# One attention and expert kernel: third softmax's exponentials as stationary f16 halves, values ahead of the last query tiles, constant products in TensorE's waits

## The reference

```python
x = x + layernorm(attention(layernorm(x), w_qkv, w_proj))
x = x + layernorm(ffn(layernorm(x), ...))       # base product + one of 8 adapters, by smallest loss

# attention, per batch and head
Q, K, V = split(x @ w_qkv);  Q = Q / 4
Q_l, K_l = means of 16 successive tokens of Q, K          # 64 landmarks
kernel1 = softmax(Q   @ K_l.T)      # 1024 x 64
kernel2 = softmax(Q_l @ K_l.T)      # 64 x 64
kernel3 = softmax(Q_l @ K.T)        # 64 x 1024, the third softmax
SV  = (kernel1 @ iterative_inv(kernel2)) @ (kernel3 @ V)  # 6 Newton steps
out = SV @ w_proj
```

## Time and profile before

| | |
|---|---|
| median of three runs | 2275.7 us (2271.61 to 2277.06) |
| the profiled execution | 2281.05 us, of which its span 2279.3 us |
| TensorE matmul busy | 2019.9 us, 89% of the span |
| DVE / ACT / POOL busy | 1471.1 (65%) / 864.9 (38%) / 700.9 us (31%) |
| mean granted TensorE clock | 0.964 of full speed |
| chain that ended last | TensorE 62%, DVE 17%, SP's queue 9%, issue 4%, ACT 3%, POOL 3%, DMA 2% |
| period of a batch | 134.5 us, from the reciprocal L1549, which starts at 94.5 us in the first batch and at 2112.2 us in the last, 15 periods later |

### The profile page before, as it was taken

One profiled execution on the slowest core, in us unless ns is written; L12 is line 12 of the kernel. 1 busy time (PEld: TensorE's weight loads), 2 busy tenths in 40 slices (PEclk: granted clock), 3 DMA queues, 4 the chain that ended last, 5 costly groups with the idle time before them and its releaser, 6 DMA issues.

```text
span 2279.3 us, 58742 instructions
## 1 busy us (share of the span) xinstructions
PE 2019.9 (89%) x24991; PEld 1307.2 (57%) x24991; DVE 1471.1 (65%) x3319; ACT 864.9 (38%) x1509; POOL 700.9 (31%) x916
## 2 busy tenths in 40 slices
PE   3888989999898998989899898989989898998945
PEld 1554747556474755647465564746657475665724
DVE  3667576766757667675766757576675757767531
ACT  3334344343433443343343434334343443334320
POOL 4153152322315232232523224251331424223051
PEclk9889999999999999999999999999999999999978
DMA  6213141221514222151422215132231513213020
GB/s 152 46 47 76 30 122 39 81 61 30 121 30 116 44 73 61 29 131 30 112 44 71 66 30 131 30 99 52 63 79 30 129 31 89 62 41 83 11 56 19
DMA packets 232972, 150.71 MB, mean 66 GB/s; under 512 B 153035, under 2 KB 203732, under 8 KB 232693
## 3 DMA queue, kind: packets, MB, share of 16 engines
q1 hardware_dynamic: 232710, 146.95, 27.5%
HBM read 36.98 MB, written 16.78 MB: 24 GB/s over the span
## 4 chain that ended last, share of the span: by engine, by line
PE 62%; DVE 17%; SPq 9%; issue 4%; ACT 3%; POOL 3%; DMA 2%; DVEq 1%; POOLq 0%; ACTq 0%
PE NS L979 11%; PE ringF L1187 9%; SPq L429 9%; PE ringF L1172 6%; PE KV L1060 5%; PE ringA L1146 5%; PE ringA L880 5%; PE ringF L1220 3%; PE ringA L1046 3%; PE ringA L1022 3%; DVE stage L1608 3%; DVE mx L1518 2%; PE ringF L880 2%; PE ringF L1222 2%; ACT E L690 2%
## 5 line engine op out<-in xcount | busy, mean ns | idle before, releaser
L1187 PE MATMUL ringF<-x,H 128*128 128x256 f16 x1536 | 237.9, 273 | 0.0
L1532 DVE TENSOR_REDUCE mx<-ringA 128x8 f32<-128x512 f32 x256 | 175.4, 685 | 89.3 <-PE ringA L1022 88.8
L682 ACT ACTIVATE E<-ringA,score_scale 128x512 f32<-128x512 f32 x256 | 175.5, 686 | 116.8 <-PE ringA L1046 116.7
L1187 PE MATMUL ringF<-H 128*128 128x128 f16 x1024 | 204.4, 220 | 1.4 <-DVE H L1619 1.4
L880 PE MATMUL ringA<-xT,wqkv 128*128 128x512 f16 x768 | 184.0, 391 | 21.2 <-ACT QS L700 11.7
L1585 DVE SCALAR_TENSOR_TENSOR X<-X,NS 128x320 f32<-128x320 f32 x160 | 78.0, 488 | 182.8 <-PE NS L979 177.7
L1518 DVE TENSOR_REDUCE mx<-ringA 128x1 f32<-128x512 f32 x256 | 160.1, 682 | 52.0 <-PE ringA L1013 51.5
L1172 PE MATMUL ringF<-wd,x2T 128*128 128x512 f16 x768 | 187.9, 384 | 6.4 <-DVE H L1619 3.1
L516 POOL TENSOR_SCALAR vtmp<-mv,eps_ffn 128x8 f32<-128x8 f32 x16 | 5.1, 316 | 612.0 <-DVE mv L1363 612.0
L690 ACT ACTIVATE E<-ringA,score_scale 128x512 f32<-128x512 f32 x256 | 158.6, 684 | 75.2 <-PE ringA L1077 75.2
L516 POOL TENSOR_SCALAR vtmp<-mv,eps_ln 128x8 f32<-128x8 f32 x32 | 9.9, 310 | 538.2 <-DVE mv L1363 538.2
(11 more groups left out here) (261 smaller groups left out, 4317.8 us busy)
## 6 DMA issues: line engine op xcount, KB each, us to landing
KS<-stage SPq DMA_DIRECT2D x384, 64.0 KB, 2.0
QS<-stage SPq DMA_DIRECT2D x384, 64.0 KB, 2.0
xin<-in_L_attn_x_dram SPq DMA_DIRECT2D x16, 1024.0 KB, 11.0
xres<-in_L_attn_x_dram SPq DMA_DIRECT2D x16, 1024.0 KB, 8.1
...
```

The costliest lines, as they stand in the source:

```text
L682: A(E[:, k % ESLOTS, :], ps[:, :], ACT.Exp, scale=score_scale[:, 0:1]).then_inc(freed["s3"].sem, 1)
L1187: ins = MM(dst, H[:, a, t, own], src, start=first and i == 0, stop=last and i >= 3, skip_group_check=True)
L1532: V_.reduce_max(mx1[:, t, 8 * h:8 * h + 8], take(b, "m1", k)[:, :].rearrange("p (a m) -> p a m", a=8), AX.X)\
```

## The change

It does seven things.

- The third softmax's exponentials come twice from ACT: once as f16 (`E16`, four slots that lie in `yout`) and once as f32 (`E`), from the same bank. POOL subtracts the first from the second and writes the low half (`exponentials_lo`).
- POOL splits the values into two f16 halves with a column of ones behind (`values16`, `V16`). The f32 `V` now lies in slots 4 to 7 of `E`.
- `sum_values` has the halves of `E` as stationary operands (128 x 128, f16) and the values as moving ones: per step 4 products of 65 columns and 4 of 33, into `KV` for the first eight steps and `NS[1]` for the last. It waits for POOL's low half and stands three steps behind the scores instead of two, and the first `gram` goes before its last two steps.
- The end: DVE copies the sums out (`values_take`, 128 x 260, twice, the first in step 11), adds two parts, and multiplies by the reciprocal of 8 columns. The big reciprocal, its product, TensorE's two transposes and the copies are gone. The small products of the denominators move from `NS[1]` to free columns of `KV`.
- `pv` 2 and 3 go after `m3` 3 and 7, `pk` 6 and 7 after `m3` 7 and 9. ACT's order follows: both values before `halves2` of the first group.
- Constant products that nobody reads (`keep_warm`, identity times 512 weight columns; `stir`, 128 columns) are put ahead of most `m3`, at the scores' steps 1, 2 and 4, in steps 11 to 14, and at the start and end of the kernel.
- ACT's `halves1` go from Newton steps 0 and 1 to 1 and 2.

```diff
@@ -114,6 +116,7 @@
...
+        E16 = yout[:, :, :].bitcast(F16).rearrange("p t c -> p (t c)").rearrange("p (s h n) -> p s h n", s=4, h=2)
...
@@ -123,8 +126,9 @@
...
-        V = sb("V", [P, T, PAIRS, HD2])
+        V16 = sb("V16", [P, T, PAIRS, 2 * HD2 + 2], F16)
         E = sb("E", [P, ESLOTS, HALF])
+        V = E[:, 4:8, :].rearrange("p k n -> p (k n)").rearrange("p (t a d) -> p t a d", t=T, a=PAIRS)
...
@@ -172,9 +179,8 @@
...
-                  + [("m3", k) for k in range(4)] + [("pk", 6), ("m3", 4), ("pk", 7)]
-                  + [("m3", k) for k in range(5, 9)] + [("pv", 2)] + [("m3", k) for k in range(9, 13)] + [("pv", 3)]
-                  + [("m3", k) for k in range(13, 16)] + [("f3", 0)])
+                  + [("m3", k) for k in range(4)] + [("pv", 2)] + [("m3", k) for k in range(4, 8)] + [("pv", 3), ("pk", 6)]
+                  + [("m3", 8), ("m3", 9), ("pk", 7)] + [("m3", k) for k in range(10, 16)] + [("f3", 0)])
...
@@ -561,6 +569,29 @@
...
+            def values16(b):
+                for k in range(4):
+                    rows = slice(2 * k, 2 * k + 2)
+                    pool.wait_ge(freed["pv"].sem, freed["pv"].at(b, k + 1))
+                    pool.sem_inc(s_apart, 1)
+                    if k == 0 and not first(b):
+                        pool.wait_ge(kv_full.sem, kv_full.at(b - 1, 2 * T))
+                        pool.sem_inc(s_apart, 1)
+                    pool.tensor_copy(V16[:, rows, :, HD2:2 * HD2], V[:, rows, :, :]).then_inc(v16.sem, 1)
+                for g in range(2):
+                    rows = slice(4 * g, 4 * g + 4)
+                    pool.wait_ge(v16.sem, v16.at(b, 4 + g))
+                    pool.sem_inc(s_apart, 1)
+                    pool.tensor_tensor(V16[:, rows, :, 0:HD2], V[:, rows, :, :], V16[:, rows, :, HD2:2 * HD2],
+                                       ALU.subtract).then_inc(v16.sem, 1)
+
+            def exponentials_lo(b):
+                for k in range(16):
+                    pool.wait_ge(freed["s3"].sem, freed["s3"].at(b, k + 1))
+                    pool.sem_inc(s_apart, 1)
+                    pool.tensor_tensor(E16[:, k % 4, 1, :], E[:, k % ESLOTS, :], E16[:, k % 4, 0, :], ALU.subtract)\
+                        .then_inc(e_lo.sem, 1)
...
             def body(b, more):
                 if not first(b):
                     norm2(b - 1)
+                values16(b)
+                exponentials_lo(b)
                 if more:
                     norm1(b + 1)
...
@@ -678,13 +711,20 @@
             def exp3(b, k):
                 ps = take(b, "s3", k)
                 if k >= ESLOTS:
-                    act.wait_ge(kv_full.sem, kv_full.at(b, k - ESLOTS + 1))
+                    act.wait_ge(e_lo.sem, e_lo.at(b, k - ESLOTS + 1))
+                elif k == 4:
+                    act.wait_ge(v16.sem, v16.at(b, 6))
+                if k >= 4:
+                    act.wait_ge(kv_full.sem, kv_full.at(b, k - 4 + 1))
+                elif k == 0 and not first(b):
+                    act.wait_ge(x2lo.sem, x2lo.at(b - 1, 2))
+                A(E16[:, k % 4, 0, :], ps[:, :], ACT.Exp, scale=score_scale[:, 0:1])
                 A(E[:, k % ESLOTS, :], ps[:, :], ACT.Exp, scale=score_scale[:, 0:1]).then_inc(freed["s3"].sem, 1)
...
@@ -752,12 +792,12 @@
                 values(b, (0, 1))
                 landmark_stack(b)
                 staged(b, (2,))
+                values(b, (2, 3))
                 if ffn:
                     halves2(b - 1, (0,))
                 staged(b, (3,))
                 if ffn:
                     halves2(b - 1, (1,))
-                values(b, (2, 3))
...
@@ -787,8 +827,8 @@
                     if k == 3:
                         exp1(b, 6)
                         exp1(b, 7)
-                    if more and k < 2:
-                        halves1(b + 1, (k,))
+                    if more and 1 <= k < 3:
+                        halves1(b + 1, (k - 1,))
...
@@ -890,6 +930,16 @@
...
+            def keep_warm(cols, times=1):
+
+                for _ in range(times):
+                    MM(NS[1][:, 0:cols], ident[:, :], wqkv[:, 0, 0, 0:cols], start=True, stop=True)
+
+            def stir(times):
+
+                for _ in range(times):
+                    MM(NS[1][:, 264:392], ident[:, :], wqkv[:, 0, 0, 0:P], start=False, stop=False, skip_group_check=True)
...
             def project(b):
+                if first(b):
+                    keep_warm(512, 10)
...
@@ -1049,24 +1101,20 @@
             def sum_values(b, k):
 
                 g, t = k // T, k % T
-                pe.wait_ge(freed["s3"].sem, freed["s3"].at(b, k + 1))
+                pe.wait_ge(e_lo.sem, e_lo.at(b, k + 1))
                 if k == 0:
-                    pe.wait_ge(freed["pv"].sem, freed["pv"].at(b, 4))
+                    pe.wait_ge(v16.sem, v16.at(b, 6))
                     if not first(b):
-                        pe.wait_ge(w_done.sem, w_done.at(b - 1, 3))
-                for i in range(2):
-                    for j in range(GP):
-                        p = g * GP + j
-                        ins = MM(KV[32 * j:32 * j + 32, (2 * g + i) * P:(2 * g + i + 1) * P], onesf[:, :] if i else V[:, t, p, :],
-                                 E[:, k % ESLOTS, j * P:(j + 1) * P], start=t == 0 and i == 0, stop=t == T - 1,
-                                 skip_group_check=True)
+                        pe.wait_ge(w_done.sem, w_done.at(b - 1, 4))
+                acc_bank = (KV, NS[1])[g]
+                for j in range(GP):
+                    p = g * GP + j
+                    cols = slice(j * P, (j + 1) * P)
+                    MM(acc_bank[:, j * VW:(j + 1) * VW], E16[:, k % 4, 0, cols], V16[:, t, p, 0:VW], start=t == 0 and j == 0,
+                       stop=False, skip_group_check=True)
+                    ins = MM(acc_bank[:, j * VW + HD2:(j + 1) * VW], E16[:, k % 4, 1, cols], V16[:, t, p, HD2:VW], start=False,
+                             stop=t == T - 1, skip_group_check=True)
                 ins.then_inc(kv_full.sem, 1)
...
@@ -1235,27 +1283,37 @@
                 project(b)
                 tokens(b, (4, 5))
                 kernel2_scores(b)
-                for k in range(4):
+                if not first(b):
+                    pe.wait_ge(freed["ss"].sem, freed["ss"].at(b - 1, 4))
+                for k in range(16):
+                    if k not in (0, 4, 8, 10):
+                        keep_warm(512)
                     maxima3(b, k)
-                tokens(b, (6,))
-                for k in range(4, 16):
-                    maxima3(b, k)
-                    if k == 4:
-                        tokens(b, (7,))
-                    if k in (8, 12):
-                        values(b, (k // 4,))
+                    if k in (3, 7):
+                        values(b, (k // 4 + 2,))
+                    if k in (7, 9):
+                        keep_warm(512, 2)
+                        tokens(b, (k // 2 + 3,))
                 if ffn_too:
                     channel_sums(b - 1)
                     hidden(b - 1, 0)
+                if first(b):
+                    keep_warm(512, 6)
                 fold3_transpose(b)
+                if first(b):
+                    keep_warm(512, 6)
                 if ffn_too:
                     for t in (1, 2, 3):
                         hidden(b - 1, t)
                 for k in range(16):
                     maxima1(b, k)
                     scores3(b, k)
-                    if k >= 2:
-                        sum_values(b, k - 2)
+                    if k in (1, 2, 4):
+                        keep_warm(512)
+                    if k >= 3:
+                        sum_values(b, k - 3)
+                    if 11 <= k < 15:
+                        stir(2)
                     if k == 6:
                         kernel2_transpose(b)
                     if ffn_too and k in (1, 3, 5, 7):
@@ -1264,11 +1322,11 @@
                         denominator_rows(b)
                     if k == 12:
                         first_iterate(b)
+                sum_values(b, 13)
+                if ffn_too:
+                    gram(b - 1, 0, range(0, T // 2))
                 for k in range(14, 16):
                     sum_values(b, k)
-                if ffn_too:
-                    gram(b - 1, 0, range(0, T // 2))
-                values_transpose(b)
                 fold1_transpose(b)
                 if ffn_too:
                     gram(b - 1, 0, range(T // 2, T))
@@ -1324,7 +1382,11 @@
             for b in range(2, B - 1):
                 body(b, True)
             body(B - 1, False)
+            pe.wait_ge(freed["ss"].sem, freed["ss"].at(B - 1, 4))
+            pe.wait_ge(x2hi.sem, x2hi.at(B - 1, 1))
+            keep_warm(512, 12)
             channel_sums(B - 1)
+            keep_warm(512, 12)
             for t in range(T):
...
             def denominator_maxima(b):
                 dve.wait_ge(ct_full.sem, ct_full.at(b, 1))
```

(35 more changed lines are left out.)

34 lines of the change are left out of this document (18 added, 16 removed).

## The result

The changed kernel takes 2308.75 us (median of 4, 2306.01 to 2309.79) against 2276.38 (2271.61 to 2277.64) for the kernel before: ratio 1.0138, 95% interval [1.0124, 1.0152]. It is slower by 32 us where 52 us of gain were forecast, and outside the range of 2190 to 2268. The profiled span is 2306.0 us, 26.7 more than before.

What follows compares the result with a forecast made beforehand. The prediction took TensorE, except where it waits, as the bound. 3.0 us a batch x 15 + 7 = 52 us off the profiled 2281.05 gave 2229, or 2224 us on the timed runs' scale; range 2190 to 2268.

Steps and rivals of the forecast that it cites:

- The working of stages 3 and 4: Third softmax and end: engine work priced and steps walked in order, 32.8 us before, gain 3.4 us a batch.
- rival F: POOL and DVE hold each other up in stage 3, about 1 us a batch: 2239 us, chance 0.08.
- the sum: Whole kernel: (3.4 - 1.1 + 0.7) = 3.0 us x 15 + 7 = 52 us of gain.
- priced `values16` at nothing: POOL's value splits: 6.7 us, done by 1010.5, four steps before exponential 4 needs the slots of `V`.
- Rival C: TensorE stands 2.2 us before stage 3, its clock falls for the first steps, costing 1.8 us: 2251 us, chance 0.18.
- The walk: Stage 3's 16 steps followed by engine durations and the ring's waiting rule; ACT longest, Newton product starts at 29.4 us.
- D: Slower: clock falls in stage 2 despite the constant products, batch loses 4.4 us: 2290 us, chance 0.11.
- SP's queue: Before stage 3: POOL's later subtraction delays SP's transpose, issues and maxima's copy, a loss of 1.1 us a batch.
- A: Likeliest case, all terms as summed, SP's delay included: 2224 us, chance 0.38.
- B: SP is not what stage 3 waits for: 5.2 us a batch, 2191 us, chance 0.17.
- -1.1 + 0.7: Stage 2: 1.1 us a batch lost against the chosen period, 0.7 counted back because the mean period is longer.
- Start and end: Constant products in the first and last waits, with the first batch's own stages: 7 us, between 0 and 10.

Runs made afterwards that it cites:

- no_reads: late_stir_mid with POOL's pass over the exponentials only writing a constant low half, reading nothing from SBUF; 2206.5 us, ratio 0.9692 to the kernel before.
- late_stir_mid: Changed kernel with value splits after DVE's four small steps, six constant products in steps 8 to 14, second `halves2` before ACT's last query-tile copy; 2252.1 us.
- v16_late: Changed kernel with POOL's passes over the values held until DVE has done its four small steps; 2297.8 us, ratio 1.0097 to the kernel before.
- no_low: Changed kernel without POOL's 16 subtractions, the second product taking the high half again; 2262.1 us, ratio 0.9925 to the kernel before.
- order_only: Kernel before with only the new order of stage 2 and its constant products; 2278.8 us, ratio 1.0012.
- halves_only: Changed kernel with the old order of stage 2 and no constant products, only the f16 halves; 2366.6 us, ratio 1.0395 to the kernel before.

## Why the prediction was wrong

Against a forecast gain of 3.0 us a batch stands a loss of 2.3. Of the 5.3 us between, 4.3 are in stages 3 and 4 (gain of 3.4 forecast, loss of 0.9 measured), 0.7 in stage 2 (loss of 0.4 forecast, 1.1 measured), and 0.2 in the rest of the batch.

The working of stages 3 and 4 held in its parts. `sum_values` runs in 0.24 us; ACT's pair takes 2 x 0.57 us back to back; POOL's pass has a median of 1.155 us; ACT has 24.0 us of work against 23.6. With the causes below taken out, no_reads has 29.7 us against the forecast 29.4, with more constant products.

**The step that failed** is the gain of 3.4 us for stages 3 and 4, by two terms: what POOL's passes cost DVE (rival F, priced at 1 us a batch and looked for in stage 3 alone), and the clock inside stage 3, which the sum held at 1.00. The whole is 33.66 - 29.70 = 3.96 us a batch in the medians: 2.34 for the first term, 1.62 for the second.

For the first, three things were missing.

- In stage 3 it costs 32.04 - 29.70 = 2.3 us a batch at full clock, of which 0.95 are the squares alone. (TensorE's own waits for POOL's passes are 8.8 us over late_stir_mid and 2.4 over no_reads, 0.4 a batch, so of the 2.3 us some 0.4 can be the shorter pass of no_reads.) Short steps wait as long as large ones: up to the rest of POOL's instruction.
- Casts and steps with a scalar wait too, though they have one input: L1587 0.53 us and L1605 1.08 instead of 0.17 and 0.23. The section of the Trainium skill cited above (SBUF — State Buffer, Who interferes with whom) lists these operations as able to take the shared ports; I had read only its rule on two inputs. Reductions from PSUM (L1595, 682 ns in the median) and products with one operand in PSUM (L1551, 692 ns) did not wait, as forecast.
- The prediction priced `values16` at nothing because it ended four steps before its reader, and never asked what DVE does meanwhile. It stood beside the four small steps that everything behind stage 2 waits for: 2.1 us, by v16_late. Of these the changed kernel could have got back only 0.6 a batch without other edits, since SP's queue is the limit right behind.

**The clock** is the second term, 33.66 - 32.04 = 1.6 us a batch. Rival C had a fall of the clock, but tied it to the wait for SP ahead of stage 3. It fell in the middle of stage 3, in 13 of the 14 middle batches, and with no DVE step held up (no_low) still in 11. The walk had 20.2 us of TensorE work in a stage 3 of 27, where it had been 26.0 of 27.2, and never asked what the gaps do to the clock. I had given F and C chances of 0.08 and 0.18 as exclusive cases; both happened, and the waits made the fall longer. Both together at their forecast prices (3.0 a batch of gain, less 1 and 1.8) would still have been faster. The slower case I had, D, laid the fall in stage 2 and did not occur: the waits of `maxima3` for DVE's `stage` fell from 55.2 us in 48 waits to 16.2 in 32, and the clock from the first `maxima3` to the transpose was 1.00 in each batch, where it had been 0.83 to 0.92. That the change came out slower, as D had it, is by another way.

**SP's queue (A against B)** was right in its mechanism, and hidden by the later transpose in the changed kernel. With the passes held back it showed: 5.47 instead of 4.60 us to `maxima1`. Against the mean batch of before, order_only gained 1.36 - 1.07 = 0.3 us in stage 2, where the prediction's -1.1 + 0.7 gave a loss of 0.4: the size of the term was 0.7 us off.

**Start and end** came out as forecast, 7 us: 2.4 us ahead of the first `maxima3`, 1.8 in the first batch, and 3.0 behind the last batch's first Newton product. The first batch's tile products took 5.34 us instead of 8.29, the last `hidden` 11.5 instead of 13.79.

Left open: no run has the new order without constant products, or these without the order, on top of halves_only, so how the 58 us between it and the changed kernel divide isn't known. Nor do the runs tell what the 0.2 us a batch behind stage 4 are.
